# Placing the first part's rows between batch 12's maxima, and batch 13's rotary additions on VectorE

## The chip, the cores and the metric

The kernel runs on one core of a Trainium2 chip. The metric is the device time of one execution in microseconds. TensorE multiplies matrices, VectorE and ScalarE do elementwise work and reductions, GpSimd does some elementwise work and issues the indirect DMAs, SyncE (SP) issues the other DMAs. Each engine takes its instructions in the order written; they meet through semaphores.

## The reference

Inputs are `x` (16 batches x 112 rows x 256) and a context (16 x 375 x 256). A cross-attention block comes first, then four layers, each of attention and a mixture of experts:

```
x = x + cross_attention(layernorm(x), ctx)
h = layernorm(x)
for l in range(4):
    a = rms(h) * ln1[l]; q, k, v = a @ wq[l], a @ wk[l], a @ wv[l]     # 16 heads, 4 key heads, 64 wide
    q, k = q*cos + rot_half(q)*sin, k*cos + rot_half(k)*sin            # rotary
    h = clip(h + softmax(q k^T / 8 + causal) v @ wo[l])
    m = rms(h) * ln2[l]; p = softmax(m @ wr[l])                        # 8 experts, top 2, weights renormed
    h = clip(h + sum over the 2 chosen e: p_e * (silu(m @ wg[l,e]) * (m @ wu[l,e])) @ wd[l,e])
out = x + h
```

All arithmetic that this change touches is float32, and positions are uint32.

## The kernel before, in words

A layer has two stages. The attention stage goes through the 16 batches, b = 0 to 15. The expert stage goes through tiles of 128 rows, sorted by expert.

**Attention, batch b.** TensorE's `iteration(b)` makes the scores of heads 0 to 7 and then of heads 8 to 15 (`scores(l, b, 0)` and `(l, b, 1)`, L838 and L843), the output projection of batch b - 1 (L893), the value projection for a pair of batches (`values`, L821, even b), the transposes of the probabilities (`turn_probs`, L858) and the query and key heads of the next pair of batches (`heads_of`, L813). VectorE takes the maxima of each half of the scores (`maxima`, L1618, followed by the negated maxima `nmax`, L1619), ScalarE computes the exponentials of that half (L1271), and VectorE scales them to probabilities (`scale_probs`, L1627 and L1628). TensorE's `values` of an even batch waits for the first half's exponentials, and its transposes wait for the scaling.

**Rotary.** Batches are taken in pairs g = b // 2, and in pair g the heads of pair g + 1 are rotated in five loads m = 0 to 4: m = 0 are the keys, 1 to 4 the queries. VectorE's `rotate` shuffles the PSUM bank into `rope` (L1598), multiplies the bank by the cosine into `qk` (L1600) and `rope` by the sine (L1602). For m = 0 it adds the two itself (L1612). For m = 1 to 4, GpSimd's `add_rotated` does it (L590) and increments `g_rope`. Loads 0 and 1 fall into the even batch, 2, 3 and 4 into the odd one. The first half of the scores of a batch waits for two of GpSimd's additions of its pair, the second half for all four.

**Routing.** The rows are routed in three parts: batches 0 to 8, 9 to 12 and 13 to 15 (`PARTS`). `RANK_STEP` is 10. For the first part, VectorE computes counts and starts in batches 10 and 11, and then the row positions in two halves: `place_first(0)` (L1723 to L1728, five operations on a 112x144 tile) at the end of batch 11 and `place_first(1)` (L1719 to L1817) in batch 12, after both maxima and ahead of the scaling. The last operation writes `pos_x` and increments `d_pos`.

**Scatter.** GpSimd then writes the rows of batches 0 to 8 to `sorted_x` in DRAM, two indirect DMAs (k = 0, 1) for each batch (`scatter_row`, L621), 18 in all. They share GpSimd's queue with the additions. In batch 12 (pair 6, load 1) it waits for `d_pos`, issues six and makes the addition of m = 1. In batch 13 it issues eight, adds m = 2, issues one, adds m = 3, issues one, adds m = 4; the two of batch 8 follow in `move_rows`, and behind them the factors of the second part (`out_factors`). SP loads the first two tiles (L417) once all 18 have landed, and TensorE transposes them in batch 14 (`turn_tile`, L921).

Of the kernel before, what the change touches and what calls it, by code (L numbers as in the profile page):

```python
# [5 lines left out]
ALU = mybir.AluOpType  # L6
# [17 lines left out]
NP = B // PB  # L24
TN = PB * S
LEAD = 5
LOADS = 5
SLOT = 128
DECS = 5
PARTS = ((0, 9), (9, 13), (13, 16))  # L30
# [84 lines left out]
def xattn_ffn(nc, x, ctx_1024, w_sim, b_sim, W_qv, b_qv, ln1_w, ln2_w, wq, wk, wv, wo, wr, wg, wu, wd, const, out):  # L115
    with ExitStack() as stack:
# [83 lines left out]
        rope = [sb(f"rope{i}", [128, GN]) for i in range(2)]  # L200
# [22 lines left out]
        def route_part(width):  # L223
# [65 lines left out]
        d_rope, d_max, d_norm, d_wo, d_lg, d_x, d_yr, d_oh, d_rt, d_pos, d_te, d_out, d_gate = (sem(n) for n in (  # L289
            "d_rope", "d_max", "d_norm", "d_wo", "d_lg", "d_x", "d_yr", "d_oh", "d_rt", "d_pos", "d_te", "d_out", "d_gate"))  # L290
# [5 lines left out]
        g_eps, g_r1, g_r2, g_rope = (sem(n) for n in ("g_eps", "g_r1", "g_r2", "g_rope"))  # L296
# [14 lines left out]
        def alone(engine):  # L311

            engine.sem_inc(passed, 1)
# [195 lines left out]
        def _(pool):  # L509
# [76 lines left out]
            def add_rotated(l, g, m):  # L586

                pool.wait_ge(d_rope, l * 40 + g * LOADS + m + 1)
                q = q_flat[g % 2][:, (m - 1) * GN:m * GN]
                pool.tensor_tensor(q, q, rope[m % 2][:, :], ALU.add).then_inc(g_rope, 1)  # L590
# [3 lines left out]
                for u in range(2):  # L594
                    pool.wait_ge(st_ye[u], (l - 1) * 16 * TILES[u] + (tiles + 1 - u) // 2 * 16 + 16)

            SOONER = (3, 7)

            def attention(l):
                for b in range(B):  # L600
                    g, odd = b // 2, b % 2
                    if odd and g + 2 < NP:
                        in_factors(l, g + 2)
                    if l and b + LEAD + 1 < B:
                        if b + LEAD + 1 == PARTS[0][1]:
                            stored(l, NT)
                        gather(l, b + LEAD + 1)
                    if g + 1 < NP:
                        for m in (2, 3, 4) if odd else (1,):
                            if b == RANK_STEP + 2:  # L610
                                scatter_first(l, 0, SOONER[0])
                            if b == RANK_STEP + 3 and m == 2:
                                scatter_first(l, *SOONER)
                            if b == RANK_STEP + 3 and m > 2:
                                scatter_row(0, SOONER[1], m - 3)
                            add_rotated(l, g + 1, m)
                    if b == PARTS[0][1]:
                        out_factors(l, 0)

            def scatter_row(h, b, k):  # L620
                pool.indirect_dma_start(  # L621
                    out=sorted_x if h == 0 else sorted_x[0:HROWS - WHOLE * SLOT, :],
                    out_offset=bass.IndirectOffsetOnAxis(ap=pos_x[:, b, k:k + 1], axis=0),
                    in_=x_sb[:, b, :], in_offset=None).then_inc(scattered[min(h, 1)], 16)
# [5 lines left out]
            def scatter_first(l, a, z):  # L630

                if a == 0:
                    pool.wait_ge(d_pos, l * NPART + 1)
                    alone(pool)
                for b in range(a, z):
                    scatter(0, b)

            def move_rows(l):

                scatter_first(l, SOONER[1] + 1, PARTS[0][1])  # L640
                for h in range(1, NPART):
                    out_factors(l, h)
                    pool.wait_ge(d_pos, l * NPART + h + 1)
                    alone(pool)
                    for b in range(*PARTS[h]):
                        scatter(h, b)
                pool.wait_ge(scattered[1], (l + 1) * 16 * (B - PARTS[0][1]) * TOPK)
                for u in range(2):
                    pool.wait_ge(m_r, l * NT + WHOLE + u - 1)
                    row = (NT - 1 - WHOLE - u) * SLOT  # L650
                    pool.dma_start(xe[u], sorted_x[row:row + SLOT, :]).then_inc(ld_late[u], 16)
# [835 lines left out]
        def _(dve):  # L1487
# [88 lines left out]
            def rows_in(step, l, b):  # L1576
                combine(step, l, b)
                dve.tensor_scalar(x_sb[:, b, 0:D], x_sb[:, b, 0:D], CLIP, -CLIP, ALU.min, ALU.max).then_inc(d_x, 1)

            def rotate(step, l, g, m, bank, between=None):  # L1580

                dve.wait_ge(p_qk, l * 40 + g * LOADS + m + 1)
                out_c = k_flat[g % 2] if m == 0 else q_flat[g % 2][:, (m - 1) * GN:m * GN]

                def tokens(t):
                    return t.rearrange("p (b t) -> p b t", b=GB)

                if m == 0 and not (isinstance(l, int) and l == 0 and g == 0):

                    dve.wait_ge(g_rope, l * 32 + g * 4)  # L1590
                if m == 2:

                    dve.wait_ge(d_rope, l * 40 + g * LOADS + 1)
                if m > 2:

                    dve.wait_ge(g_rope, l * 32 + g * 4 + m - 2)
                alone(dve)
                dve.stream_shuffle(rope[m % 2][:, :], ps[:, bank, 0:GN], [(i + 16) % 32 for i in range(32)]).then_inc(step.sem, 1)  # L1598
                step.n += 1
                dve.tensor_tensor(tokens(out_c), tokens(ps[:, bank, 0:GN]), bc(cst[:, C_COS:C_COS + S], 1, [128, GB, S]), ALU.mult)  # L1600
                dve.wait_ge(step.sem, step.base + step.n)
                ins = dve.tensor_tensor(tokens(rope[m % 2][:, :]), tokens(rope[m % 2][:, :]),  # L1602
                                        bc(cst[:, C_SIN:C_SIN + S], 1, [128, GB, S]), ALU.mult)
                if m == 0:
                    if between and g > 1:
                        ins.then_inc(step.sem, 1)
                        step.n += 1
                        between(2 * g - 3)
                        dve.wait_ge(step.sem, step.base + step.n)
                    else:  # L1610
                        step(ins)
                    ins = dve.tensor_tensor(out_c, out_c, rope[0][:, :], ALU.add)  # L1612
                ins.then_inc(d_rope, 1)

            def maxima(step, l, b, p):
                dve.wait_ge(p_sc, l * 32 + 2 * b + p + 1)
# [4 lines left out]
            def layer(l, last_layer):  # L1621
# [206 lines left out]
                for b in range(B):  # L1828
                    g, odd = b // 2, b % 2
                    if b:  # L1830
                        maxima(step, l, b, 0)
                        if l and b + LEAD < B:
                            rows_in(step, l, b + LEAD)
                        if b == MID_STEP:
                            gates(0)
                            choose(1)
                        maxima(step, l, b, 1)
# [39 lines left out]
                    if b == RANK_STEP:  # L1877
                        copy_ranks(0, 3)
                        tiles_of_first()
                    if b == RANK_STEP + 1:  # L1880
                        place_first(0)
                    if b == MID_STEP:
                        copy_ranks(1, 3)

# [170 lines left out]
RANK_STEP = PARTS[0][1] + 1  # L2055
# [29 lines left out]
```

## Time and profile before

| | |
|---|---|
| median of 3 runs | 1905.0 us (1904.42 to 1906.77) |
| the profiled execution | 1908.5 us, its span 1906.7 us |
| TensorE busy | 1837.7 us, 96% of the span |
| VectorE busy | 1288.2 us, 68% |
| ScalarE busy | 948.8 us, 50% |
| GpSimd busy | 543.9 us, 29% |
| TensorE's granted clock, mean | 0.994 of full speed |

Times in timelines count from the start of the span. PE is TensorE, PEld its weight loads, DVE is VectorE, ACT is ScalarE, POOL is GpSimd, and L12 is line 12 of the kernel. Neighbouring instructions on one engine overlap by some 0.1 us where the second doesn't depend on the first. A number in brackets at the end of a row is the idle time of the engine ahead of it, with what ended that idle time. Four layers repeat the same pattern some 435 us apart.

### The profile page before, as it was taken

The numbers are of one execution on the slowest core, as the hardware profiler recorded it, in microseconds if no ns is written. First come the engines' busy times: TensorE is split into PE (matmuls) and PEld (weight loads), VectorE is DVE, ScalarE is ACT, GpSimd is POOL, SyncE is SP. The second block draws the span as 40 slices with busy tenths as digits, with TensorE's granted clock in tenths as the row PEclk, the third lists the DMA queues.
The fourth block names the chain that finished last, engine by engine and source line by source line (L and its number), as shares of the span: only waits on it lengthen the run. The fifth ranks groups of instructions, "written<-read, shape, count | busy, mean of one in ns | idle before, by whom it ended". The sixth has DMA issues, their size and how long they took to land.

```text
span 1906.7 us, 36659 instructions
## 1 busy us (share of the span) xinstructions
PE 1837.7 (96%) x10612; PEld 1358.1 (71%) x10613; DVE 1288.2 (68%) x3173; ACT 948.8 (50%) x3625; POOL 543.9 (29%) x721
## 2 busy tenths in 40 slices
PE   5999999999999999999999999999999999999995
PEld 4888888766667888766667888765667888765663
DVE  3676778764467788764467788864466788865456
ACT  4546776732225777642224777642224777652221
POOL 3752212540032233531032332531022332520014
PEclk9999999999999999999999999999999999999998
DMA  6323220245662330236663331236663431135666
GB/s 159 113 86 110 101 100 2 84 121 146 147 161 80 133 130 6 84 104 147 148 156 94 115 119 39 78 86 149 146 166 78 142 119 44 42 89 148 147 163 172
DMA packets 255292, 212.37 MB, mean 111 GB/s; under 512 B 145826, under 2 KB 226420, under 8 KB 255028
## 3 DMA queue, kind: packets, MB, share of 16 engines
q1 hardware_dynamic: 240808, 174.74, 33.7%
q0 software_dynamic: 13952, 35.33, 6.4%
q8 instruction: 82, 1.34, 0.3%
q14 instruction: 70, 0.57, 0.1%
q10 hardware_dynamic: 380, 0.38, 0.1%
HBM read 137.32 MB, written 73.05 MB: 110 GB/s over the span
## 4 chain that ended last, share of the span: by engine, by line
PE 72%; DVE 10%; ACT 8%; issue 3%; POOL 2%; SPq 2%; DMA 2%; POOLq 0%; DVEq 0%; ACTq 0%
PE ps L927 23%; PE ps L953 12%; ACT parena L1271 8%; PE ps L813 8%; PE ps L893 6%; PE ps L869 3%; PE ps L858 3%; PE ps L843 3%; PE ps L821 3%; PE ps L795 2%; DVE rmax L1618 2%; DVE rope L1598 2%; DVE rope L1602 2%; PE ps L921 2%; POOL qk L590 1%
## 5 line engine op out<-in xcount | busy, mean ns | idle before, releaser
L927 PE MATMUL ps<-arena,xeT 128*128 x1120 | 509.4, 593 | 0.0
L1271 ACT ACTIVATE parena<-ps,nmax 112x112 f32<-112x112 f32 x1024 | 345.5, 388 | 115.9 <-DVE nmax L1619 115.9
L927 PEld LDWEIGHTS ps<-arena,xeT 128*128 128x128 f32 x1120 | 210.3, 190 | 193.2 <-issue 187.0
L590 POOL TENSOR_TENSOR qk<-qk,rope 128x448 f32<-128x448 f32 x128 | 146.2, 1142 | 547.0 <-DVE rope L1602 546.7
L1320 ACT ACTIVATE parena<-ps,er 128x512 f32<-128x512 f32 x140 | 96.2, 687 | 383.5 <-PE ps L927 378.8
L813 PE MATMUL ps<-xnT,wqk_s 128*128 128x224 f32 x1280 | 273.5, 357 | 0.0
L569 POOL DMA_INDIRECT y_in<-sorted_y,pos x114 | 111.2, 976 | 500.1 <-DMA sorted_y<-tarena 396.4
L1271 ACT ACTIVATION_READ_ACCUMULATOR parena<-ps,nmax 112x1 f32 x1024 | 247.0, 241 | 0.0
L893 PE MATMUL ps<-wo_s,oT 128*112 128x256 f32 x1024 | 237.9, 385 | 1.3 <-issue 1.3
L813 PEld LDWEIGHTS ps<-xnT,wqk_s 128*128 128x128 f32 x1280 | 233.5, 191 | 3.1
L1894 DVE SCALAR_TENSOR_TENSOR parena<-parena,ps 128x512 f32<-128x512 f32 x140 | 96.1, 686 | 184.6 <-ACT parena L1320 184.6
L893 PEld LDWEIGHTS ps<-wo_s,oT 128*112 128x112 f32 x1024 | 175.7, 177 | 42.9 <-issue 2.0
L621 POOL DMA_INDIRECT sorted_x<-x_sb,pos_x x128 | 127.7, 998 | 188.0 <-DVE pos_x L1817 154.9
L1618 DVE TENSOR_REDUCE rmax<-ps 112x8 f32<-112x896 f32 x128 | 139.0, 1086 | 49.2 <-PE ps L843 48.4
L1310 ACT ACTIVATE xeT<-ps,ln2T 128x128 f32<-128x128 f32 x280 | 87.4, 365 | 165.6 <-PE ps L921 164.2
L953 PE MATMUL ps<-arena,tarena 128*128 x640 | 153.2, 382 | 2.8 <-issue 2.0
L1280 ACT ACTIVATE tarena<-ps 112x448 f32<-112x448 f32 x256 | 130.3, 584 | 33.9 <-PE ps L858 33.2
L1628 DVE TENSOR_TENSOR parena<-parena,rrec 112x896 f32<-112x896 f32 x128 | 139.8, 1092 | 4.4
L1896 DVE SCALAR_TENSOR_TENSOR parena<-parena,er,ps 128x512 f32<-128x512 f32 x140 | 104.6, 747 | 54.7 <-PE ps L927 54.2
L1284 ACT ACTIVATE oT<-ps 128x448 f32<-128x448 f32 x128 | 69.6, 545 | 123.7 <-PE ps L869 123.5
L953 PEld LDWEIGHTS ps<-arena,tarena 128*128 128x128 f32 x640 | 119.1, 195 | 15.7 <-issue 4.7
L858 PE MATMUL ps<-cst,parena 112*112 112x112 f32 x1024 | 119.6, 259 | 6.1 <-DVE parena L1628 4.9
(207 smaller groups left out, 2789.5 us busy)
## 6 DMA issues: line engine op xcount, KB each, us to landing
sorted_y<-tarena SPq DMA_DIRECT2D x140, 128.0 KB
xe<-sorted_x SPq DMA_DIRECT2D x132, 130.0 KB, 2.5
arena<-in_L_ffn_wg_dram SPq DMA_DIRECT2D x32, 512.0 KB, 3.7
arena<-in_L_ffn_wu_dram SPq DMA_DIRECT2D x32, 512.0 KB, 4.6
arena<-in_L_ffn_wd_dram SPq DMA_DIRECT2D x32, 512.0 KB, 5.6
hid_d<-tarena SPq DMA_DIRECT2D x240, 64.0 KB
tarena<-hid_d SPq DMA_DIRECT2D x60, 256.0 KB, 2.8
hid_d<-parena SPq DMA_DIRECT2D x240, 64.0 KB
```

The costliest lines, as they stand in the source:

```text
L569: pool.indirect_dma_start(out=y_in[:, b % 2, k, :], out_offset=None, in_=sorted_y[0:FIRST * SLOT, :] if b < PARTS[0][1] else sorted_y, in_ ...
L590: pool.tensor_tensor(q, q, rope[m % 2][:, :], ALU.add).then_inc(g_rope, 1)
L621: pool.indirect_dma_start(out=sorted_x if h == 0 else sorted_x[0:HROWS - WHOLE * SLOT, :], out_offset=bass.IndirectOffsetOnAxis(ap=pos_x[: ...
L813: last = pe.matmul(ps[:, bank, x * TN:x * TN + TN], wqk_s[:, k, n, :], xnT[:, g % 2, k, :], start=(k == 0), stop=(k == KD - 1))
L858: last = pe.transpose(ps[0:S, 4 + j, i * S:i * S + S], prob[:, p * 8 + j * 4 + i, :], ident[0:S, 0:S])
L893: last = pe.matmul(ps[0:S, 6, 0:D], oT[:, p, i * S:i * S + S], wo_s[:, 4 * p + i, :], start=(p == 0 and i == 0), stop=(p == 1 and i == 3))
L927: last = pe.matmul(ps[:, bank, :], xeT[u][:, k, :], w[:, bass.ds(e * 1024 + k * 512, 512)], start=(k == 0), stop=(k == KD - 1))
L953: last = pe.matmul(ps[:, 6, u * D:u * D + D], chunk, wd_s[:, bass.ds(e * 1024 + c * D, D)], start=(c == 0), stop=(c == 3))
L1271: last = act.activation(prob[:, n, :], ps[0:S, bank, h * S:h * S + S], ACT.Exp, bias=nmax[:, b % 2, n:n + 1], scale=SCALE, accum_out=rsum[ ...
L1280: act.activation(probT[:, unit, :], ps[0:S, 4 + unit % 2, 0:GN], ACT.Copy).then_inc(a_pt, 1)
L1618: step(dve.tensor_reduce(rmax[:, hs].rearrange("p (n h) -> p n h", n=2), heads(b, p), AX_X, ALU.max))
L1628: dve.tensor_tensor(prob[:, hs, :], prob[:, hs, :], bc(rrec[:, hs], 2, [S, 8, S]), ALU.mult).then_inc(d_norm, 1)
```

## The change

On VectorE, `place_first(0)` leaves the end of batch 11 and stands between the two calls of `maxima` of batch 12. In batch 13 the additions of loads 2, 3 and 4 for pair 7 leave GpSimd. VectorE makes each of them behind its own sine product: it waits for the product's increment of `d_rope`, and the addition increments `g_rope`. Ahead of the first of them it waits until GpSimd's addition of load 1 is done, so that the increments come in order. GpSimd issues six scatters in batch 12 and the other twelve in a row behind the addition of load 1.

```diff
-            SOONER = (3, 7)
+            SOONER = 3
...
                         for m in (2, 3, 4) if odd else (1,):
                             if b == RANK_STEP + 2:
-                                scatter_first(l, 0, SOONER[0])
-                            if b == RANK_STEP + 3 and m == 2:
-                                scatter_first(l, *SOONER)
-                            if b == RANK_STEP + 3 and m > 2:
-                                scatter_row(0, SOONER[1], m - 3)
-                            add_rotated(l, g + 1, m)
+                                scatter_first(l, 0, SOONER)
+                            if not (odd and g + 1 == NP - 1):
+                                add_rotated(l, g + 1, m)
...
             def move_rows(l):
-                scatter_first(l, SOONER[1] + 1, PARTS[0][1])
+                scatter_first(l, SOONER, PARTS[0][1])
...
                 ins.then_inc(d_rope, 1)
+                if g == NP - 1 and m > 1:
+
+                    if m == 2:
+                        dve.wait_ge(g_rope, l * 32 + g * 4 + 1)
+                    dve.wait_ge(d_rope, l * 40 + g * LOADS + m + 1)
+                    dve.tensor_tensor(out_c, out_c, rope[m % 2][:, :], ALU.add).then_inc(g_rope, 1)
...
                         maxima(step, l, b, 0)
                         if l and b + LEAD < B:
                             rows_in(step, l, b + LEAD)
+                        if b == RANK_STEP + 2:
+                            place_first(0)
...
-                    if b == RANK_STEP + 1:
-                        place_first(0)
```

## Rows read from the trace of the kernel before

**Rows 1.** the page, part 4: the chain that ended last, by engine
```profile
PE 72%; DVE 10%; ACT 8%; issue 3%; POOL 2%; SPq 2%; DMA 2%; POOLq 0%; DVEq 0%; ACTq 0%
```

**Rows 2.** waits of TensorE: tile, line, releaser; us in total, times, longest
```profile
PE ps L838 <- POOL qk L590: 6.5, 9, 0.8
...
PE ps L858 <- DVE parena L1628: 4.9, 4, 1.2
...
PE ps L821 <- ACT parena L1271: 3.2, 4, 0.8
```

**Rows 3.** timeline of TensorE, layer 0: start, length, engine, line, operation, tiles, shapes [idle]
```profile
326.83 0.96 PE L843 MATMUL ps<-qk 64*112 64x112 f32 x16
...
334.12 1.98 PE L821 MATMUL ps<-wv_s,xnT 128*112 128x256 f32 x8 [0.79 <-ACT parena L1271]
...
335.94 0.93 PE L858 MATMUL ps<-cst,parena 112*112 112x112 f32 x8
...
360.97 0.40 PE L838 MATMUL ps<-rows_b,causal_b 64*112 64x256 bf16 x4 [0.80 <-POOL qk L590]
...
365.30 0.95 PE L858 MATMUL ps<-cst,parena 112*112 112x112 f32 x8 [1.21 <-DVE parena L1628]
```

**Rows 4.** timeline of VectorE, layer 0, batch 12
```profile
327.73 0.88 DVE L1723 TENSOR_TENSOR route<-route,whole 112x144 f32<-112x144 f32 x1
...
328.64 0.31 DVE L1724 TENSOR_TENSOR route<-route,first 112x144 f32<-112x144 f32 x1
...
329.94 1.09 DVE L1618 TENSOR_REDUCE rmax<-ps 112x8 f32<-112x896 f32 x1
...
331.07 0.17 DVE L1619 TENSOR_SCALAR nmax<-rmax 112x8 f32<-112x8 f32 x1
...
334.66 1.09 DVE L1628 TENSOR_TENSOR parena<-parena,rrec 112x896 f32<-112x896 f32 x1
```

**Rows 5.** timeline of VectorE, layer 0, batches 13 and 14
```profile
348.64 1.09 DVE L1628 TENSOR_TENSOR parena<-parena,rrec 112x896 f32<-112x896 f32 x1
...
355.17 1.33 DVE L1602 TENSOR_TENSOR rope<-rope,cst 128x448 f32<-128x448 f32 x1
...
357.51 1.45 DVE L1602 TENSOR_TENSOR rope<-rope,cst 128x448 f32<-128x448 f32 x1
...
359.46 1.09 DVE L1618 TENSOR_REDUCE rmax<-ps 112x8 f32<-112x896 f32 x1
...
360.58 0.38 DVE L1619 TENSOR_SCALAR nmax<-rmax 112x8 f32<-112x8 f32 x1
...
364.06 1.09 DVE L1628 TENSOR_TENSOR parena<-parena,rrec 112x896 f32<-112x896 f32 x1
```

**Rows 6.** timeline of GpSimd, layer 0, batches 11 to 14
```profile
327.31 1.13 POOL L590 TENSOR_TENSOR qk<-qk,rope 128x448 f32<-128x448 f32 x1 [0.56 <-DVE rope L1602]
...
348.31 0.93 POOL L621 DMA_INDIRECT sorted_x<-x_sb,pos_x  x1 [0.30 <-issue]
...
357.33 1.13 POOL L590 TENSOR_TENSOR qk<-qk,rope 128x448 f32<-128x448 f32 x1
...
359.79 1.13 POOL L590 TENSOR_TENSOR qk<-qk,rope 128x448 f32<-128x448 f32 x1
...
362.33 0.93 POOL L621 DMA_INDIRECT sorted_x<-x_sb,pos_x  x1 [0.30 <-issue]
```

**Rows 7.** timeline of VectorE, layer 0, key rotation of pair 1
```profile
160.01 0.62 DVE L1602 TENSOR_TENSOR rope<-rope,cst 128x448 f32<-128x448 f32 x1
...
160.66 0.63 DVE L1612 TENSOR_TENSOR qk<-qk,rope 128x448 f32<-128x448 f32 x1
...
161.21 0.65 DVE L1598 STREAM_SHUFFLE rope<-ps 128x448 f32<-128x448 f32 x1
```

**Rows 8.** timelines of SP's queue and of TensorE, layer 0, first tiles
```profile
364.90 0.80 SPq L417 DMA_DIRECT2D xe<-sorted_x  x2
...
368.05 0.62 PE L921 MATMUL ps<-cst,xe 128*128 128x128 f32 x4
```

## The prediction, written before the result

> **What bounds the kernel now.** I read the page first. TensorE makes 72% of the chain that ended last, VectorE 10% and ScalarE 8% [rows 1]. So a microsecond is saved only where TensorE stands still, and the question is which wait ends last there. The list of TensorE's waits has three entries that belong to the stretch of the change: scores that wait for a GpSimd rotary addition (9 times, up to 0.8 us), transposes that wait for VectorE's scaling of probabilities (4 times, up to 1.2), and value projections that wait for ScalarE's exponentials (4 times, up to 0.8) [rows 2]. Then I read the timelines of layer 0 around batches 12 to 14. Layers 1 to 3 repeat them with the same waits to within 0.05 us, so each term below counts four times.
>
> TensorE's timeline [rows 3] gives the places. In batch 12, `values` starts at 334.12 after 0.79 us of idleness, and the transposes follow at 335.94 with no wait. In batch 14, the second half of the scores starts at 360.97 after 0.80 us of waiting for GpSimd, and the transposes at 365.30 after 1.21 us of waiting for VectorE. Batch 13 has no TensorE wait. VectorE's timeline [rows 4] shows why the first wait exists: the scores of heads 0 to 7 end at 326.83 + 0.96 = 327.79, but their maxima start only at 329.94, since the first half of the placing (from 327.73) stands in front of them. In batch 13 [rows 5] VectorE is late again: the maxima of batch 14 start at 359.46, directly behind other VectorE work. The sine products of 355.17 and 357.51 took 1.33 and 1.45 us, and the small `nmax` operation of 360.58 took 0.38.
>
> **The held operations.** An undisturbed sine product takes 0.62 us [rows 7], an undisturbed `nmax` operation 0.17 (that of 331.07 [rows 4]). Each long one ends close behind a GpSimd addition: GpSimd's of 357.33 ended at 358.46 and VectorE's product at 358.96; GpSimd's of 359.79 ended at 360.92 and the `nmax` operation at 360.96 [rows 5, 6]. The first placing operation took 0.88 us where its neighbour on the same tile took 0.31; it ended at 328.61, and the GpSimd addition of 327.31 at 328.44 [rows 4, 6]. I read all of them as VectorE held until GpSimd's addition is done.
>
> **Part 1: place_first(0) goes between the two maxima of batch 12.** It issues the same five VectorE operations and no DMA. In the old place they cost 329.94 - 327.73 = 2.21 us, of which 0.88 - 0.31 = 0.57 is holding (bounds 0 and 0.57). In the new place no GpSimd addition runs, so they cost 1.64.
> - The first maxima start behind their scores. I give them the 0.15 us that the transposes of 365.30 took behind the end of the scaling (364.06 + 1.09) [rows 3, 5]: 327.94 instead of 329.94, 2.0 earlier. The exponentials for which `values` waits end 2.0 earlier too. TensorE itself is free at 334.12 - 0.79 = 333.33, so `values` gains the whole 0.79.
> - VectorE's work up to the probabilities of this half is the same set of operations: it gains 0.57 and loses 327.94 - 327.73 = 0.21 of new idleness. The scaling of 334.66 moves 0.36 earlier, ends at 335.39, and the transposes start at 335.54 instead of 335.94. This now ends last, and TensorE waits 0.4 us there. **Gain 0.40.**
> - What hides the inserted 1.64 us is ScalarE's work on the first half. It lasts from the end of `nmax` (331.24) to the start of `values` (334.12), 2.9 us; the second maxima with their `nmax` take 1.2 and the placing 1.64, together 2.8. They still start 0.4 earlier than now. If ScalarE came to wait for them, nobody waits for it, since TensorE needs the second half only behind further transposes. Without that cover the price is at most 1.64.
> - GpSimd's scatters of batch 12 wait for the positions, which come 0.36 earlier. From the transposes to the end of batch 13 TensorE doesn't wait, so everything moves by 0.40.
>
> **Part 2: in batch 13 VectorE makes the three additions.** Each waits for its own sine product by a semaphore. The key rotation has such a pair: product at 160.01, addition at 160.66, next shuffle at 161.21 [rows 7]. An operation of 0.62 that nothing waits for lets the next start about 0.54 behind its own start (the addition of 0.63 does after 0.55). So an addition costs 1.20 - 0.54 = 0.66, and three cost **1.98**. Queued behind each wait are the logits copy, the next rotation and the maxima of batch 14. What goes is the holding: 1.33 - 0.62 = 0.71 and 1.45 - 0.62 = 0.83, together **1.54** (bounds 0 and 1.54), and behind them 0.38 - 0.17 = **0.21** at `nmax`. The exponentials, VectorE's scaling of 364.06 and TensorE's transposes of 365.30 follow `nmax` without slack. So these transposes start 0.40 + 1.54 + 0.21 - 1.98 = **0.17 us earlier**, and so does everything behind them.
>
> TensorE's wait of 0.80 for GpSimd disappears: the last addition starts at 357.51 - 0.40 - 0.71 + 3 x 0.66 = 358.4 and ends at 359.0, before TensorE is free at 360.17 - 0.40 = 359.77. That is no gain, since the next thing that TensorE needs are probabilities from VectorE's chain. The 0.80 joins the 1.21 in one longer wait.
>
> **GpSimd** keeps one addition in batch 12 and then issues twelve scatters in a row. Its set of operations up to the last scatter shrinks by three additions, 3 x 1.13 = 3.4 us, and starts 0.36 earlier, so the last scatter ends up to 3.8 ahead of 362.33 + 0.93 = 363.26 [rows 6]. If the denser VectorE work lengthened each of the twelve by half a sine product, 0.31, that would be 3.7, and it would end where it ends now. SP's load of the first tiles waits for all scatters. It went out at 364.90 in 0.80 for two, and TensorE read the first tile at 368.05 without a wait [rows 8]. To spare there is less than 368.05 - 365.70 = 2.35 us, so the load must not get later, and it doesn't. Behind the scatters GpSimd computes the second part's factors, now at about 360 beside VectorE's `nmax` and small operations. Their effect is unseen: 0, or one hold at most as long as the longest above (0.83). I take 0, nearer to the small size of the operation; the upper end goes into the range as 3.3 us.
>
> **The sum.** 4 layers x 0.17 = 0.7 us less. The profiled execution took 1908.5 us, 1906.7 of span and 1.8 around it; it becomes 1907.8 with a span of 1906.0. It stood 3.5 above the median of the runs, 1905.0, and the same difference gives 1904.3. A measurement of this kernel tells a change of about 0.2% (3.8 us) from none, so the forecast is no measurable change.
>
> **A rule against the change.** The rows first: at 348.64 VectorE began a product of two SBUF inputs 0.33 us after a scatter had begun at 348.31, and took 1.09, as that of 334.66 did, which had begun before any scatter [rows 4 to 6]. So the scatter didn't hold it. In the Trainium skill, the page "SBUF — State Buffer", section "SBUF: two separate sides", says that a VectorE operation with two SBUF inputs and a GpSimd operation that reads SBUF exclude one another for a whole instruction. By that rule the sine products are rightly held by GpSimd's additions, as the trace shows; but a scatter, if reading its indices counts, would hold the three new additions too, which the row of 348.64 doesn't show. What it would give is the third rival.
>
> **Rivals.**
> 1. *All of TensorE's waits go.* If the probabilities of batch 14 came in time, 0.79 + 0.80 + 1.21 = 2.80 per layer were saved, 11.2 in all: 1893.8. Half of it, with help from positions, factors and first tiles that come up to 4 us earlier, gives 1899.4. Each wait's named cause is indeed removed or moved. Against it: VectorE's sum from 327.73 to 359.46 hardly shrinks. Chance 0.13 for more than 3.8 us.
> 2. *The change doesn't relieve the placing.* If its first operation is 0.88 long by itself, every later step is 0.57 worse: 0.40 a layer lost, 1.6 in all: 1906.6. Against it: the neighbour's 0.31. Chance 0.07.
> 3. *Slower: scatters hold the additions.* GpSimd scatters without a pause while VectorE adds. An addition that waits for the scatter in progress loses 0 to 0.93, half on average: 3 x 0.47 = 1.4 a layer; 2.8 at most. The place is the start of batch 14's maxima. At 1.4 the sum is 4 x (1.4 - 0.17) = 4.9: 1909.9; at 2.8 it is 1915.5. It decides from 3.8 / 4 + 0.17 = 1.1 us a layer. The 1.54 + 0.21 of holding that stays for a cause other than the additions does the same at the same place (1911.3) and is counted here. Against it: the row of 348.64. Chance 0.12.
>
> **How the numbers follow.** Forecast 0.68 (1904.3, its own range 1901.5 to 1907.6, the upper end by the factors' hold), rivals 0.13, 0.07 and 0.12. Faster by over 0.2%: 0.13. Within: 0.68 + 0.07 = 0.75. Slower: 0.12. The range takes in the forecast, rival 2 and the near ends of the others: 1900.0 to 1908.8.
>
> **What would show it.** In layer 0: maxima of batch 12 at about 327.9; no wait of `values`, and one of about 0.4 us for VectorE at the transposes behind it; three additions of 0.63 us on VectorE in batch 13 with sine products of 0.62; batch 14's scores without a wait for `qk`, then one wait of 2 us or more for the probabilities; the first tiles' load up to 4 us earlier. The prediction is wrong if the new additions are longer than 0.63, if batch 14's maxima start over 0.5 us from 359.5, or if the expert tiles, where I expect nothing, change their length.

## The result, and the profile after

The changed kernel takes 1911.3 us in the median (1907.98 to 1914.62) against 1905.4 for the kernel before on the same chip (1904.42 to 1906.77). The ratio is 1.0026, with a 95% interval of 1.0016 to 1.0036. It is slower by 5.9 us in the medians (5.0 by the ratio), outside the predicted range, on the side that had a chance of 0.12. The profiled execution took 1911.86 us with a span of 1910.0; TensorE's mean granted clock in it is 0.992, before it was 0.994. The other executions show 0.991 to 0.995 after. They have no timeline, so everything below is read from one execution of each kernel. The fastest of the changed kernel (1908.0 us) has 0.995, so the loss found below need not have come in all four layers of every execution.

**Where the time went.** I measured fixed stretches of TensorE's timeline, from anchor to anchor: the first counting matmul (`ps<-oh_b,low_b`) of batch 10, that of batch 14, the last part, the expert tiles. The startup ahead of layer 0 varies by some 5 us between runs, so absolute starts say nothing. Only one stretch differs clearly: the others differ by up to 0.5 us and the part behind the last anchor by 1.1, no more than among the later runs. In us from batch 10's to batch 14's counting:

| layer | 0 | 1 | 2 | 3 | mean |
|---|---|---|---|---|---|
| before | 59.91 | 59.96 | 59.97 | 59.97 | 59.95 |
| after | 61.31 | 61.35 | 61.69 | 61.36 | 61.43 |

The sum of the four differences is 5.9 us, the whole change in the medians. This stretch is the measure of all that follows. In layer 0 it begins at 310.11 before and at 306.63 after; "at +t" below is a time behind that anchor.

The page after, part 4, the chain that ended last by engine. It answers to [rows 1]: TensorE has gained two points, and SP's queue has lost its two.

```profile
PE 74%; DVE 11%; ACT 7%; issue 3%; POOL 3%; DMA 2%; SPq 0%; POOLq 0%; DVEq 0%; ACTq 0%
```

The list of TensorE's waits, after: tile, line, releaser, us in total, times, longest. It answers to [rows 2]. The wait for ScalarE at `values` (3.2 us, 4 times) has left it, and the waits for GpSimd have halved. The wait for VectorE at the transposes has grown from 4.9 to 11.2 us, and its longest from 1.2 to 2.3.

```profile
PE ps L855 <- DVE parena L1631: 11.2, 8, 2.3
...
PE ps L835 <- POOL qk L590: 3.2, 5, 0.7
```

TensorE's timeline after, layer 0, answering to [rows 3] (start, length, operation, idle time ahead in brackets):

```profile
331.95 0.98 PE L855 MATMUL ps<-cst,parena 112*112 112x112 f32 x8 [0.39 <-DVE parena L1631]
...
356.17 0.40 PE L835 MATMUL ps<-rows_b,causal_b 64*112 64x256 bf16 x4
...
357.30 1.98 PE L890 MATMUL ps<-wo_s,oT 128*112 128x256 f32 x8
...
361.58 1.31 PE L855 MATMUL ps<-cst,parena 112*112 112x112 f32 x8 [2.30 <-DVE parena L1631]
...
363.05 3.08 PE L818 MATMUL ps<-wv_s,xnT 128*112 128x256 f32 x8
...
365.96 0.63 PE L918 MATMUL ps<-cst,xe 128*128 128x128 f32 x4
```

All of the forecast's waits are there. The transposes of batch 14 start at 361.58 - 306.63 = +54.95, before at 365.30 - 310.11 = +55.19: 0.24 us earlier. Up to that point the change is a gain. What comes behind is longer: `values`, the same eight matmuls as the row of 329.68 with 1.89 us, takes 3.08 (3.16, 3.19 and 3.12 in layers 1 to 3, where the transposes behind the wait still take 0.95).

TensorE's timeline after, layer 0, batch 12, the same operation:

```profile
329.68 1.89 PE L818 MATMUL ps<-wv_s,xnT 128*112 128x256 f32 x8
```

The windows of the kernel after show why. Columns: stretch, its length, busy us (instructions) of PE, PEld, DVE, ACT and POOL, granted clock, DMA share, GB/s.

```profile
357.30:359.27 1.97, 1.97 (x10) 1.33 (x8) 1.65 (x7) 1.97 (x13) 1.50 (x3) 1.00 0.21 62
...
359.27:361.58 2.31, 0.01 (x2) 0.03 (x1) 2.20 (x5) 2.28 (x15) 0.00 (x0) 1.00 0.47 115
...
362.00:363.00 1.00, 1.00 (x8) 1.00 (x7) 0.17 (x2) 1.00 (x7) 0.00 (x0) 0.52 0.00 0
...
364.00:365.00 1.00, 1.00 (x4) 0.77 (x3) 0.25 (x1) 0.25 (x2) 0.00 (x0) 0.50 0.00 0
...
366.00:367.00 1.00, 1.00 (x11) 1.00 (x10) 0.00 (x0) 0.60 (x1) 0.00 (x0) 1.00 0.00 0
...
361.58:365.96 4.38, 4.38 (x18) 3.71 (x19) 1.77 (x4) 2.67 (x12) 0.00 (x0) 0.61 0.00 0
```

The same work in the kernel before, from the transposes to the first tile:

```profile
365.30:368.05 2.75, 2.75 (x19) 2.46 (x19) 1.77 (x4) 2.54 (x12) 0.00 (x0) 1.00 0.36 97
```

TensorE worked at a granted clock of 1.00 up to 359.27 and then stood still for 2.3 us. Shortly after it is at work again (at about 362.0 in layer 0) the granted clock falls to 0.50, 1.2 instead of 2.4 GHz, until past 365, and TensorE, busy all the time in both, takes 4.38 us for what took 2.75: 1.63 us more. From there the distance to the counting matmul is the same as before. So the layer gains 0.24 and loses 1.64 (6.36 us from the transposes to the counting instead of 4.72), together 1.40, the difference in layer 0. In the kernel before, no stretch of four microseconds between startup and the last 20 us has a clock under 0.97; after, the windows behind these four waits do.

The startup of the kernel before does have such a place. TensorE waits 3.10 us for an input there, and works at half clock behind it:

```profile
42.67 1.53 PE L724 MATMUL ps<-cst,arena 125*128 125x125 f32 x6 [3.10 <-DMA arena<-in_ctx_dram]
```

```profile
42.00:46.00 4.00, 3.33 (x12) 2.94 (x13) 0.58 (x2) 1.71 (x4) 0.27 (x1) 0.50 1.04 236
```

The Trainium skill describes such a clock in "TensorE: Matmul & The Clock Gate", section "Part 1: The HAM clock gate": one of two levels is granted, by how busy the array has recently been. The rows agree on the two levels.

VectorE's timeline after, layer 0, batches 12 and 13, answering to [rows 4, 5]:

```profile
324.44 1.09 DVE L1621 TENSOR_REDUCE rmax<-ps 112x8 f32<-112x896 f32 x1 [0.24 <-PE ps L840]
...
325.65 0.30 DVE L1726 TENSOR_TENSOR route<-route,whole 112x144 f32<-112x144 f32 x1
...
350.20 0.63 DVE L1616 TENSOR_TENSOR qk<-qk,rope 128x448 f32<-128x448 f32 x1
...
351.90 0.61 DVE L1599 TENSOR_TENSOR rope<-rope,cst 128x448 f32<-128x448 f32 x1
...
352.55 0.62 DVE L1616 TENSOR_TENSOR qk<-qk,rope 128x448 f32<-128x448 f32 x1
...
354.82 0.62 DVE L1616 TENSOR_TENSOR qk<-qk,rope 128x448 f32<-128x448 f32 x1
...
355.95 1.09 DVE L1621 TENSOR_REDUCE rmax<-ps 112x8 f32<-112x896 f32 x1
```

The placing operation is 0.30 long where it was 0.88, the sine product 0.61 where it was 1.33, and the three additions last 0.62 to 0.63. The maxima of batch 14 start at +49.32, before at 359.46 - 310.11 = +49.35.

GpSimd's and SP's timelines after, layer 0, answering to [rows 6, 8]: one scatter of batch 13, the last scatter, and SP's load of the first tiles.

```profile
345.12 1.47 POOL L618 DMA_INDIRECT sorted_x<-x_sb,pos_x  x1 [0.30 <-issue]
...
356.57 0.93 POOL L618 DMA_INDIRECT sorted_x<-x_sb,pos_x  x1 [0.30 <-issue]
```

```profile
359.26 0.80 SPq L417 DMA_DIRECT2D xe<-sorted_x  x2
```

The last scatter ends at +50.87 instead of +53.15, 2.3 us earlier, and the load goes out at +52.63 instead of +54.79, 2.2 earlier. The forecast allowed 0 to 3.8 for the last scatter.

### The profile page after: what moved, and what is told of

Same layout as the page of the kernel before. It is cut to its first block, busy times and chain, and to the rows that moved or that the text cites. A ratio compares the mean times of both kernels' runs of the same rounds, so it can differ in the third digit from the quotient of the medians.

```text
span 1910.0 us, 36667 instructions
## 1 busy us (share of the span) xinstructions
PE 1844.8 (97%) x10612; PEld 1363.1 (71%) x10613; DVE 1288.2 (67%) x3185; ACT 948.8 (50%) x3625; POOL 535.2 (28%) x709
## 4 chain that ended last, share of the span: by engine, by line
PE 74%; DVE 11%; ACT 7%; issue 3%; POOL 3%; DMA 2%; SPq 0%; POOLq 0%; DVEq 0%; ACTq 0%
PE ps L924 23%; PE ps L950 12%; PE ps L810 8%; ACT parena L1268 7%; PE ps L890 6%; PE ps L866 3%; PE ps L855 3%; PE ps L840 3%; PE ps L818 3%; DVE rmax L1621 2%; PE ps L792 2%; PE ps L918 2%; DVE rope L1595 2%; POOL qk L590 2%; DVE rope L1599 1%
## 5 line engine op out<-in xcount | busy, mean ns | idle before, releaser
L590 POOL TENSOR_TENSOR qk<-qk,rope 128x448 f32<-128x448 f32 x116 | 132.7, 1144 | 546.3 <-DVE rope L1599 546.2
L618 POOL DMA_INDIRECT sorted_x<-x_sb,pos_x x128 | 132.6, 1036 | 203.4 <-DVE pos_x L1820 168.6
L855 PE MATMUL ps<-cst,parena 112*112 112x112 f32 x1024 | 120.2, 260 | 12.4 <-DVE parena L1631 11.2
```

What stands on the lines that cost most here:

```text
L618: pool.indirect_dma_start(out=sorted_x if h == 0 else sorted_x[0:HROWS - WHOLE * SLOT, :], out_offset=bass.IndirectOffsetOnAxis(ap=pos_x[: ...
L855: last = pe.transpose(ps[0:S, 4 + j, i * S:i * S + S], prob[:, p * 8 + j * 4 + i, :], ident[0:S, 0:S])
```

## The experiments

The theory: TensorE's one long wait of 2.3 us brings the clock down, and that is the whole loss. The rival: one of the two parts is slow by itself, through an engine that delays another, and the clock only comes along with it. Every kernel ran beside the kernel before on its own chip. "Stretch" is the mean over the four layers of the stretch in the table, 59.95 us before and 61.43 after.

### Each part alone

**Part 1 alone**, in the kernel before:

```diff
                         maxima(step, l, b, 0)
+                        if b == RANK_STEP + 2:
+                            place_first(0)
...
-                    if b == RANK_STEP + 1:
-                        place_first(0)
```

> Part 1 alone: place_first(0) stands between batch 12's maxima, while GpSimd keeps its additions and the interleaved scatters of batch 13. Clock theory (the change merges two TensorE waits of batch 14 into one of 2.3 us, TensorE's granted clock falls to half behind it and costs 1.64 us a layer): the two waits of about 0.80 and 1.21 stay apart, the granted clock stays at 1.00 in batch 14, and only the gain of batch 12 is left, 4 x 0.40 = 1.6 us: about 1903.8 against 1905.4. Rival (the placing's new place is what costs): about 1908 or more, and the stretch from batch 10's to batch 14's counting matmuls longer than the 59.95 us of before.

Measured: 1908.4 us (1905.35 to 1912.39), ratio 1.0014 (1.0005 to 1.0023), stretch 60.55, 0.60 more than before. The numbers are those of the rival (about 1908, a longer stretch). The clock theory's 1903.8 missed, though the clock stayed at 1.00 and the two waits apart, as it said. So part 1 by itself costs something that has nothing to do with the clock. TensorE's timeline, layer 0, batch 14:

```profile
357.16 0.40 PE L838 MATMUL ps<-rows_b,causal_b 64*112 64x256 bf16 x4 [1.52 <-POOL qk L590]
...
361.48 0.95 PE L858 MATMUL ps<-cst,parena 112*112 112x112 f32 x8 [1.21 <-DVE parena L1628]
```

The wait for GpSimd's additions is 1.52 instead of 0.80, and the transposes start at +55.76 instead of +55.19. VectorE's and GpSimd's timelines of the same run, batches 12 and 13, show where it starts:

```profile
331.79 1.09 DVE L1628 TENSOR_TENSOR parena<-parena,rrec 112x896 f32<-112x896 f32 x1
...
343.78 1.09 DVE L1628 TENSOR_TENSOR parena<-parena,rrec 112x896 f32<-112x896 f32 x1
...
350.31 0.63 DVE L1602 TENSOR_TENSOR rope<-rope,cst 128x448 f32<-128x448 f32 x1
...
352.55 0.67 DVE L1598 STREAM_SHUFFLE rope<-ps 128x448 f32<-128x448 f32 x1
```

```profile
332.25 1.46 POOL L621 DMA_INDIRECT sorted_x<-x_sb,pos_x  x1 [0.30 <-issue]
...
344.20 1.48 POOL L621 DMA_INDIRECT sorted_x<-x_sb,pos_x  x1 [0.30 <-issue]
...
351.24 1.14 POOL L590 TENSOR_TENSOR qk<-qk,rope 128x448 f32<-128x448 f32 x1
```

The shuffle of load 4 writes the half of `rope` that the addition of load 2 reads, and starts only when that addition has ended (351.24 + 1.14 = 352.38, shuffle 352.55). The addition stands in GpSimd's queue behind eight scatters of batch 13. VectorE is earlier by part 1, GpSimd isn't: two scatters that began while VectorE's scaling ran lasted 1.46 and 1.48 us instead of 0.94. VectorE then waits for GpSimd. In the complete change this can't happen, since there VectorE makes that addition itself.

**Part 2 alone**: the changed kernel, with `place_first(0)` back at the end of batch 11.

```diff
-                        if b == RANK_STEP + 2:
-                            place_first(0)
...
+                    if b == RANK_STEP + 1:
+                        place_first(0)
```

> Part 2 alone: the three additions on VectorE and the scatters in a row, with place_first(0) back at the end of batch 11. Clock theory: batch 13 costs VectorE 1.98 - 1.54 - 0.21 = 0.23 us more, TensorE's wait in batch 14 is one of 0.80 + 1.21 + 0.23 = 2.2 us, the granted clock falls to about 0.5 behind it and costs another 1.6: 4 x 1.87 = 7.5 us more, about 1913. Rival (the additions cost only VectorE's time, and the clock falls for a reason in batch 12): 4 x 0.23 = 0.9 more, about 1906.3, with the granted clock at 1.00 in batch 14.

Measured: 1913.2 us (1909.5 to 1917.23), ratio 1.0038 (1.0026 to 1.005), stretch 61.77, 1.82 more than before. TensorE's timeline, layer 0, batch 14:

```profile
363.68 1.71 PE L855 MATMUL ps<-cst,parena 112*112 112x112 f32 x8 [2.32 <-DVE parena L1631]
...
365.56 2.56 PE L818 MATMUL ps<-wv_s,xnT 128*112 128x256 f32 x8
```

The expectation held, in all four layers (waits of 2.31 and 2.32). The wait and the slow matmuls come with the additions. The parts' losses, 0.60 and 1.82 a layer, don't add up to the 1.48 of both: with part 2 in place part 1 is a gain of 0.34, since part 2 takes away the wait for GpSimd that part 1 alone runs into.

### The wait filled

The changed kernel, with two matmuls that nobody reads ahead of batch 14's wait. The output stays as it is; they only keep TensorE at work.

```diff
                         out_project(b - 1, 1)
+                        if b == B - 2:
+                            for _ in range(2):
+                                pe.matmul(ps[:, 4, 0:GN], cst[:, 0:128], cst[:, 0:GN], start=True, stop=True)
```

> The changed kernel with two extra matmuls of 128x448 float32 (some 0.75 us each, an estimate from four passes over 448 columns as in the 128x256 ones) on TensorE in batch 14, right behind the second half of the out projection, into a PSUM bank that the next transposes overwrite; the output is unchanged. They fit into the wait of 2.3 us, so no work of the path moves. Clock theory: the remaining wait is about 0.8 us, the granted clock stays at 1.00, the value projections take 1.9 us and not 3.1, and 4 x 1.64 = 6.6 us come back: about 1904.7. Rival (the 1.5 us behind the wait come from something else than the idle TensorE): no change, about 1911.

Measured: 1904.3 us (1902.65 to 1906.17), ratio 0.9991 (0.9982 to 1.0), stretch 59.77. TensorE's timeline, layer 0, batch 14:

```profile
359.90 1.67 PE L1014 MATMUL ps<-cst 128*128 128x448 f32 x4
...
362.36 0.95 PE L855 MATMUL ps<-cst,parena 112*112 112x112 f32 x8 [0.80 <-DVE parena L1634]
...
363.38 1.89 PE L818 MATMUL ps<-wv_s,xnT 128*112 128x256 f32 x8
```

This separates the two theories. Nothing came earlier, and what was added is of no use to the output, but the wait of 2.3 us is cut into work and 0.80, the clock stays at 1.00, the transposes take 0.95 and `values` 1.89. The stretch falls by 1.66 a layer, which is the 1.64 of the clock. Against the kernel before, 59.95 - 59.77 = 0.18 a layer is left. That is close to the 0.17 of the prediction only as a mean: layers 0, 1 and 3 save 0.24 to 0.28 and layer 2 loses 0.04.

### Useful work in the wait

The changed kernel, with the value projections of batch 14 ahead of its transposes rather than behind them:

```diff
                         if not odd:
-                            if more:
-                                values(l, g, 0)
+                            values(l, g, 0)
...
                     else:
-                        values(l, g, 0)
                         for T in range(2):
```

> The changed kernel with the value projection of batches 14 and 15 ahead of batch 14's transposes instead of behind them (as in the other even batches); it needs only the exponentials of the first half, which end 1.4 us before the transposes can start. Clock theory: 1.8 us of work go into the wait, transposes start some 0.4 us later, so 1.4 us a layer are saved, and the clock no longer falls, 1.64 more: 4 x 3.0 = 12 us, about 1899. Rival (the slow stretch does not come from the idle time): only 4 x 1.4 = 5.6 us, about 1905.7, with the granted clock still near 0.5 behind the transposes.

Measured: 1905.0 us (1901.51 to 1907.77), ratio 0.9995 (0.9986 to 1.0004), stretch 59.35. The number is near the rival's 1905.7, but its condition is not met: the clock holds. The stretch is 61.43 - 59.35 = 2.08 a layer shorter than in the changed kernel, 1.64 of it the clock's; of the further 1.4 that was expected only 0.42 came, and nothing of it shows in the median beside the filled kernel's. TensorE's timeline, layer 0, batch 14:

```profile
362.58 1.98 PE L818 MATMUL ps<-wv_s,xnT 128*112 128x256 f32 x8 [0.85 <-ACT parena L1266]
...
366.76 0.98 PE L855 MATMUL ps<-cst,parena 112*112 112x112 f32 x8 [0.69 <-DVE parena L1629]
```

`values` now waits 0.85 for ScalarE, and the transposes of the second half wait 0.69 for VectorE's scaling. I had moved 1.9 us of TensorE's work into a wait of 2.3 and counted it as saved, where VectorE's chain ends last in both orders.

### Eight runs that tell little

Four variants ran on two other chips, each on both. There the kernel before itself takes 1941.7 and 1940.7 us. It has no trace there, but the traces of the variants show one cause in all of them: in nearly every layer ScalarE stands still in batch 13, for 2 to 5 us at a time, and for 5.5 to 7 behind batch 15. TensorE waits for it, and the clock falls. ScalarE's timeline in layer 0 of the kernel before with early `values`:

```profile
353.86 0.98 ACT L1278 ACTIVATE tarena<-ps 112x448 f32<-112x448 f32 x2 [4.96 <-remote]
```

The stretch is 60.4 to 68.3 us in the layers of these runs, whatever the variant. The stall lies inside it and covers the question. "Last on GpSimd" is the changed kernel with the addition of load 4 back on GpSimd, behind ten scatters:

```diff
-                            if not (odd and g + 1 == NP - 1):
+                            if odd and g + 1 == NP - 1:
+                                if m == 4:
+                                    scatter_first(l, SOONER, 8)
+                                    add_rotated(l, g + 1, m)
+                            else:
                                 add_rotated(l, g + 1, m)
...
-                scatter_first(l, SOONER, PARTS[0][1])
+                scatter_first(l, 8, PARTS[0][1])
...
-                if g == NP - 1 and m > 1:
+                if g == NP - 1 and m in (2, 3):
```

"Placing, six" is part 1 alone with `SOONER = (3, 6)` in place of `(3, 7)`, so that six scatters instead of eight stand ahead of the addition of load 2. "Values" is the reordering shown above.

The kernel before with early `values`, on one chip and on the other:

> The kernel before, with the value projection of batches 14 and 15 ahead of batch 14's transposes. The wait of 1.21 us is filled; what ends last then is the scaling of the second half, which in the trace of before ends at 367.6 where the transposes of that half start at 368.51. So 0.8 us a layer at most are saved, 3.2 in all: 1902.2, the stretch from batch 10's to batch 14's counting matmuls 59.2 us instead of 59.95. If the first tile's load, which leaves little to spare in this kernel, comes too late, the gain is 0.3 to 0.5 a layer less. It tells how much of the changed kernel's gain from the same edit (59.35) is owed to the change.

> The kernel of e5 again, for the same reason: the value projection early in the kernel before saves up to 0.8 us a layer (59.2 us from batch 10 to batch 14), 0.3 to 0.5 less if the first tile's load comes too late.

Ratios 0.9994 (0.998 to 1.0008) and 0.9997 (0.9983 to 1.0011): no difference.

Last on GpSimd:

> The changed kernel with the addition of load 4 back on GpSimd, behind ten of the twelve scatters; VectorE keeps those of loads 2 and 3. VectorE reaches batch 14's maxima 0.66 us earlier, so TensorE's wait for the probabilities shrinks from 2.30 to about 1.65. Clock theory: 0.17 + 0.66 = 0.8 us a layer are saved against before if the clock does not fall (the kernel with the placing alone had a wait of 1.52 and no fall): 4 x 0.8 = 3.3, about 1902.1; if the clock still falls behind 1.65 us, 4 x 1.6 = 6.5 more, about 1908.6. Rival (GpSimd's addition holds VectorE again, as the two long sine products did): the addition comes behind VectorE's last product, so only the small nmax operation could be held, 0.2 a layer.

> The kernel of e7 again, because in e7's runs ScalarE stood still for about 5 us in batch 13 of every layer without any engine holding it, in all four kernels, and that covered what was asked. Expected as before: TensorE's wait for batch 14's probabilities about 1.65 us, the granted clock at 1.00 there, the stretch from batch 10 to batch 14 59.1 us and 3.3 us less than the kernel before; 1908 or more above a 1905 of before if the clock falls behind 1.65 us.

Ratios 1.0013 (0.9999 to 1.0027) and 1.0014 (1.0 to 1.0027).

Last on GpSimd, with early `values`:

> The same with the value projection ahead of batch 14's transposes. In the changed kernel that edit brought the stretch from batch 10 to batch 14 from 59.77 (clock kept by filling) to 59.35 us; with VectorE 0.66 earlier it should be about 58.7, so 4 x 1.25 = 5 us less than before: about 1900.5. If the scaling of the second half or the first tile's load binds instead, 59.2 and 1902.5.

> The kernel of e8 again, for the same reason: the stretch from batch 10 to batch 14 about 58.7 us, 5 us less than the kernel before.

Ratios 1.0008 (0.9996 to 1.0021) and 1.0005 (0.9989 to 1.0021).

Placing, six:

> The placing alone, with six instead of eight scatters ahead of GpSimd's addition of load 2. In the kernel with the placing alone (60.55 us from batch 10 to batch 14, 0.6 more than before) VectorE's shuffle of load 4 waited 1.7 us for that addition, since scatters in front of it took up to 1.48 instead of 0.94 where they met a two-input VectorE operation. Theory (the scatters' length is what costs): with two scatters fewer the addition is 2.5 us earlier, the wait is gone, and the gain of batch 12 is left: 59.5 to 59.9, 1903.6 to 1905.4. Rival (the placing itself costs later in the batch): still about 60.5 and 1908.

> The kernel of e9 again, for the same reason: 59.5 to 59.9 us from batch 10 to batch 14 if the eight scatters ahead of GpSimd's addition of load 2 are what costs in the placing alone (0 to 1.6 us less than the kernel before); still 60.5 and 2.4 us more if it is the placing itself.

Ratios 0.9984 (0.9973 to 0.9995) and 0.997 (0.9951 to 0.999). I don't read a verdict out of any of the eight. Three of the variants ran again beside a kernel before of 1906.3 us, and all three ratios came out on the other side of 1. The kernel before with early `values` wasn't run there.

### The same on a chip without that stall

**Placing, six:**

> The kernel of e9 (placing alone, six scatters ahead of the addition of load 2), where the kernel before takes 1905 and not 1941 us, if this chip gives that: 59.5 to 59.9 us from batch 10 to batch 14 and 1903.6 to 1905.4 if the eight scatters ahead of the addition are what costs 0.6 us a layer in the placing alone; still 60.5 and about 1908 if it is the placing itself.

Measured: 1916.9 us (1913.24 to 1920.42), ratio 1.0051 (1.0038 to 1.0064), stretch 61.07. GpSimd's timeline, layer 0, batch 13:

```profile
353.40 1.14 POOL L590 TENSOR_TENSOR qk<-qk,rope 128x448 f32<-128x448 f32 x1 [0.89 <-DVE rope L1602]
```

The number missed both expectations, but the mechanism named for part 1 is confirmed: the addition of load 2 now waits for its product and not for scatters, and the transposes of batch 14 start at 363.88 - 309.85 = +54.03, 1.16 earlier than before. But the scatters that were moved behind it end later. SP's queue and TensorE's timeline, layer 0:

```profile
366.19 0.80 SPq L417 DMA_DIRECT2D xe<-sorted_x  x2
```

```profile
368.30 0.98 PE L921 MATMUL ps<-cst,xe 128*128 128x128 f32 x4 [1.51 <-DMA xe<-sorted_x]
```

The load goes out at +56.34, 1.55 later than before, and the first tile is waited for. In layers 1 and 3 the clock also fell, behind two waits one after the other (1.22 and 1.48 us in layer 1, 1.22 and 1.44 in layer 3), and the stretch from batch 14 to batch 15 took 31.10 and 31.43 us instead of the 28.61 and 28.84 of before. Layers 0 and 2 have the same two waits, even slightly longer (1.22 and 1.51, 1.22 and 1.52), and no fall. So the length of the waits alone doesn't settle it. Layer 1, the wait and the window behind it:

```profile
803.48 1.09 PE L921 MATMUL ps<-cst,xe 128*128 128x128 f32 x4 [1.48 <-DMA xe<-sorted_x]
```

```profile
805.00:809.00 4.00, 4.00 (x25) 2.37 (x23) 0.81 (x5) 2.92 (x9) 0.00 (x0) 0.53 0.02 6
```

The expectation missed the end because it left out the scatters' own deadline.

**Last on GpSimd:**

> The kernel of e7 (additions of loads 2 and 3 on VectorE, that of load 4 on GpSimd), under the same condition: one TensorE wait of about 1.65 us in batch 14. With the clock at 1.00, 59.1 us from batch 10 to batch 14 and 3.3 us less than before. If the clock falls behind 1.65 us too, 60.7 and 3 us more than before.

Measured: **1901.8 us** (1900.18 to 1908.83), ratio 0.9983 (0.9974 to 0.9992), stretch 59.02 (59.01 to 59.03 in all four layers). GpSimd's and TensorE's timelines, layer 0:

```profile
354.19 1.13 POOL L590 TENSOR_TENSOR qk<-qk,rope 128x448 f32<-128x448 f32 x1 [0.27 <-DVE rope L1603]
```

```profile
360.24 0.95 PE L859 MATMUL ps<-cst,parena 112*112 112x112 f32 x8 [1.65 <-DVE parena L1635]
...
361.26 1.89 PE L822 MATMUL ps<-wv_s,xnT 128*112 128x256 f32 x8
```

One addition less on VectorE makes its chain earlier and the wait 1.65 instead of 2.30. Behind 1.65 us of idleness `values` takes 1.89 and the granted clock doesn't fall, in any of the four layers. Of the other executions, which have no timeline, the slowest (1908.8 us) shows a mean clock of 0.993 where the profiled one has 0.996, so it isn't shown that this holds every time.

**Last on GpSimd, with early `values`:**

> The kernel of e8 (the same with the value projection ahead of batch 14's transposes), under the same condition: about 58.7 us from batch 10 to batch 14, 5 us less than before, no fall of the clock.

Measured: **1899.3 us** (1898.45 to 1903.18), ratio 0.9966 (0.9953 to 0.9979), stretch 58.49. This beats both kernels: 6.5 us under the one before by the ratio, 1.46 a layer in the stretch. How much of it the change has to do with isn't known, because the kernel before with early `values` ran only on the two chips with the stall. TensorE's timeline, layer 0:

```profile
361.12 1.98 PE L822 MATMUL ps<-wv_s,xnT 128*112 128x256 f32 x8 [0.22 <-ACT parena L1270]
...
365.17 0.98 PE L859 MATMUL ps<-cst,parena 112*112 112x112 f32 x8 [0.41 <-DVE parena L1633]
```

The single wait has become two of 0.22 and 0.41 us.

## Why the prediction was wrong

**The step that failed** is the sentence "The 0.80 joins the 1.21 in one longer wait". The joined wait was foreseen, its size too ("2 us or more"), and it was priced at nothing beyond its own length, as if TensorE worked on afterwards as before. It costs a lowered clock: 4.38 us for 2.75 us of work in layer 0, 1.64 to 1.66 a layer, 6.6 in all. Up to batch 14's transposes the four layers are 0.7 us shorter together, as forecast, and 6.6 - 0.7 is the measured 5.9. Filling the wait gave that time back with nothing else changed, so this is shown and not only argued. No rival held a fall of the clock. The mean clock of 0.994 said nothing of the layers, since all that is missing in it lies in the startup and the last 20 us. But the wait of 3.10 us in the startup, with half clock behind it, was there to be read, and the prediction didn't look at what followed a long wait.

The forecast of 1904.3 and the filled kernel's 1904.3 agree partly by luck, since they sum over layers that differ.

**What held, by its own steps.**
- Part 1's gain of 0.40: the wait of `values` is gone, the transposes behind it wait 0.39 and start at +25.32 instead of +25.83, 0.51 earlier (0.50 and 0.52 in layers 1 and 3), and the placing's first operation is 0.30 long. Rival 2 is out. Layer 2 gains only 0.17: the first maxima of batch 12 start 0.36 later there behind the same scores, and why isn't known. The filled kernel and the one with early `values` have it too.
- The holding: the sine products are 0.61 once GpSimd adds nothing beside them.
- The additions at 0.66 each: from the sine product to the operation behind the addition it took 1.26, 1.20 and 1.19, where 0.54 is usual without one, so they cost 0.72, 0.66 and 0.65. Their length was 0.62 to 0.63.
- The maxima of batch 14, forecast at about 359.5 of before's time, came at +49.32, which is 359.43.
- The sum at the transposes of batch 14, 0.17 earlier: 0.24 measured in layer 0, 0.27 in layers 1 and 3, and 0.07 later in layer 2, 0.18 in the mean.
- GpSimd's factors beside VectorE's small operations, taken at 0, cost nothing that shows: the transposes are not late.

**The rivals.** Rival 3, the only slower one, reached the right side for a reason that isn't there: the additions ran beside scatters at 0.63 us. Its second cause, holding that stays, has the measured 1911.3 to the digit, and that is chance: the sine products are 0.61. The exclusion exists in the other direction. A scatter that starts while VectorE works on two SBUF inputs lasts until about 0.8 us behind VectorE's end (344.70 + 1.09 = 345.79 and 345.12 + 1.47 = 346.59). All scatters average 1036 ns after, 998 before. The prediction bounded this lengthening at 0.31 each. Single scatters exceed it (by 0.54 over the usual 0.93), but the twelve of layer 0 together are only 1.6 us longer, 0.13 each. The page "SBUF — State Buffer" of the Trainium skill, section "SBUF: two separate sides", has whichever starts first keep the port; the scatters' rows fit that, and the product of [rows 5] that ran on behind a scatter's start doesn't, nor does the addition of 352.55, which began 0.11 us behind a scatter and took 0.62. Rival 1 has part of the truth: with the load-4 addition on GpSimd and early `values`, an edit that it didn't have, 1.46 us a layer of the 2.80 can be had.

**Not additive.** The prediction summed the parts as if each kept its value alone. Part 1 alone loses 0.60 by a wait of VectorE for a GpSimd addition that stands behind scatters, which part 2 removes. The forecast for part 1 looked at TensorE and VectorE and not at what GpSimd's queue then holds up.

**What stays open.** From which length of a wait the clock falls isn't settled: in this place it didn't behind 1.65 us and did behind 2.30 to 2.33, in all eight layers of two kernels. It did in two layers of four behind 1.22 and 1.48 or 1.44 in a row, and didn't in any behind 1.52 to 1.54 and 1.21 in a row (part 1 alone). Whether the wait must be unbroken, or only the idleness close together counts, isn't shown: the filling took away both. What early `values` alone are worth in the kernel before isn't known without the stall. Why ScalarE stands still on two other chips isn't known. What ends last in the fastest version is VectorE's scaling of the second half (the wait of 0.41), and moving that earlier wasn't tried.

## What to carry to other kernels

Two short waits that merge into one long one need not cost the same as their sum: before pricing a merged TensorE wait at its length, look whether the trace has another of about that length, in the startup too, and what the granted clock is behind it. If it falls there, or if there is none to look at, put the following matmuls at half clock into the range (here 1.6 us for each fall). A wait that must stay can be cut with work, even useless work, as the filled kernel shows. When work is moved between two engines that share tiles, follow the last instruction of each queue: GpSimd's additions set VectorE's next shuffle, and the last scatter sets the first tile.

## What the runs showed of the hardware

- Behind 2.30 us without a matmul, TensorE's granted clock went from 1.00 to 0.50 and eight value matmuls from 1.89 to 3.08 us; behind 1.65 us it stayed at 1.00, in the profiled executions.
- The same two waits, 1.22 and about 1.5 us with 2.9 us of work in between, had a fall to 0.50 behind them in two layers of one execution and none in the other two.
- A scatter of 0.94 us takes 1.46 to 1.48 when it starts during VectorE's scaling, which itself keeps its 1.09. Four lengthened scatters in batch 13 of the changed kernel's layer 0 began during a VectorE product or addition on two SBUF inputs, and each ended 0.80 to 0.82 us behind it.
- The kernel before took 1905.7 and 1906.3 us on two chips and 1941.7 and 1940.7 on two others, where the traces of four variants show ScalarE standing still at two places of a layer, for 2 to 5 us at a time and for about 7.
